# A cross-attention layer: the scores in stretches of two, three and three pairs, and what moves with them

## The reference, cut to what matters

```python
# x (8, 64, 512); ctx (8, 1601, 512); mask (8, 1601); 16 heads of 32
q = split_heads(layernorm(x) @ q_w.T + q_b)
k = split_heads(ctx @ k_w.T + k_b)
v = split_heads(ctx @ v_w.T + v_b)
scores = where(mask > 0, -inf, einsum("bhqd,bhkd->bhqk", q, k) / sqrt(32))
x = x + merge_heads(softmax(scores) @ v)                      # cross attention

h = layernorm(x)
q = h @ W_q.T
x = x + (q @ h.T) @ h                                         # per batch of 64 tokens

h = layernorm(x)
top_v, top_i = top_k(h @ gate_w + gate_b, 2)                  # 2 of 8 experts
x = x + sum over experts of weight * (relu(h @ w1[e] + b1[e]) @ w2[e] + b2[e])
```

## Time and profile before

| | us |
|---|---|
| median of 3 runs | 1223.51 |
| lowest and highest of them | 1223.32, 1225.69 |
| the profiled execution, its own time | 1225.0 |
| its span, from first to last instruction | 1223.2 |
| PE busy in the span | 1200.1 (98%) |
| DVE, ACT, POOL busy | 842.1, 697.7, 213.6 |

### The profile page before, as it was taken

How to read it: one execution, slowest core, us unless ns; L and a number is a source line. 1 busy time by engine, 2 the same in 40 slices (tenths; PEclk the granted TensorE clock), 3 DMA queues, 4 the chain that set the end, 5 groups by cost and what they waited for, 6 DMA issues and landing times.

```text
span 1223.2 us, 25806 instructions
## 1 busy us (share of the span) xinstructions
PE 1200.1 (98%) x10197; PEld 1122.2 (92%) x10197; DVE 842.1 (69%) x2154; ACT 697.7 (57%) x1266; POOL 213.6 (17%) x239
## 2 busy tenths in 40 slices
PE   7999999999999999999999999999999999999997
PEld 6899999999999999999999999999879898899896
DVE  6656666566665666666566666777789887887876
ACT  6455545645654564564455456455656676687772
POOL 0004202410420251051023105101112000000012
PEclk9999999999999999999999999999999999999999
DMA  8102200220220031022003002200318777768663
GB/s 286 55 1 92 85 1 2 95 82 1 92 84 1 3 118 58 1 92 84 1 28 119 31 2 92 98 1 2 114 69 285 245 253 262 251 226 283 234 206 122
DMA packets 61059, 127.19 MB, mean 104 GB/s; under 512 B 3644, under 2 KB 21192, under 8 KB 60824
## 3 DMA queue, kind: packets, MB, share of 16 engines
q1 hardware_dynamic: 58776, 118.97, 28.6%
q0 software_dynamic: 2176, 6.72, 1.5%
HBM read 120.01 MB, written 14.32 MB: 110 GB/s over the span
## 4 chain that ended last, share of the span: by engine, by line
PE 90%; DVE 6%; ACT 2%; DMA 1%; issue 1%; SPq 0%; DVEq 0%
PE ptp L948 26%; PE work L948 22%; PE work L1335 8%; PE ptp_pv L1118 6%; PE work L986 6%; PE work L1337 3%; PE ptp L1358 2%; PE ptp L1361 2%; PE ptp L1359 2%; PE ptp L1360 2%; PE ptp L1362 2%; DVE kk_lo L1498 2%; ACT kk_hi L687 1%; PE work L1101 1%; DVE pt L1617 1%; PE work L955 1%
## 5 line engine op out<-in xcount | busy, mean ns | idle before, releaser
L948 PE MATMUL ptp<-vw_hi,cx_hi 128*128 128x256 f32 x832 | 242.2, 291 | 0.0
L948 PE MATMUL ptp<-vw_lo,cx_hi 128*128 128x256 f32 x832 | 235.7, 283 | 0.0
L948 PE MATMUL ptp<-vw_hi,cx_lo 128*128 128x256 f32 x832 | 235.7, 283 | 0.0
L948 PE MATMUL work<-cx_hi,kw_hi 128*128 128x400 f32 (+1 forms) x504 | 175.8, 349 | 1.3 <-DVE cx_lo L1519 1.3
L948 PE MATMUL work<-cx_hi,kw_lo 128*128 128x400 f32 (+1 forms) x504 | 173.6, 344 | 0.0
L948 PE MATMUL work<-cx_lo,kw_hi 128*128 128x400 f32 (+1 forms) x504 | 173.4, 344 | 0.0
L948 PEld LDWEIGHTS ptp<-vw_hi,cx_hi 128*128 128x128 f32 x832 | 159.5, 192 | 13.8 <-issue 12.7
L948 PEld LDWEIGHTS ptp<-vw_lo,cx_hi 128*128 128x128 f32 x832 | 159.6, 192 | 0.0
L948 PEld LDWEIGHTS ptp<-vw_hi,cx_lo 128*128 128x128 f32 x832 | 159.6, 192 | 0.0
L1498 DVE SCALAR_TENSOR_TENSOR kk_lo<-work,biasT,kk_hi 128x400 fp32r<-128x400 f32 (+1 forms) x128 | 79.5, 633 | 115.0 <-ACT kk_hi L687 114.9
L687 ACT ACTIVATE kk_hi<-work,biasT 128x400 fp32r<-128x400 f32 (+1 forms) x128 | 75.1, 595 | 127.2 <-PE work L948 124.5
(11 more groups left out here) (301 smaller groups left out, 2601.0 us busy)
## 6 DMA issues: line engine op xcount, KB each, us to landing
w1raw<-in_w SPq DMA_DIRECT2D x32, 1024.0 KB, 6.1
w2raw<-in_w SPq DMA_DIRECT2D x32, 1024.0 KB, 5.3
raw<-in_ctxT SPq DMA_DIRECT2D x31, 832.0 KB, 6.5
pr<-in_mask SPq DMA_DIRECT2D x8, 800.5 KB, 4.4
xrow<-x_rows SPq DMA_DIRECT2D x7, 256.0 KB, 5.3
y_rows<-y_out_rows POOLq DMA_DIRECT2D x7, 256.0 KB, 3.7
xs<-in_x SPq DMA_DIRECT2D x1, 1024.0 KB, 9.8
qwraw<-in_qwT SPq DMA_DIRECT2D x1, 1024.0 KB, 8.8
```

What stands on the lines that cost most here:

```text
L948: last = pe.matmul(dst, lhs(i, c), rhs(j, c), start=(c == 0 and (i, j) == (0, 0)), stop=(c == n - 1 and (i, j) == (1, 0)))
```

## The change

- The eight score pairs of a half are in stretches of 2, 3 and 3 pairs in place of 2, 2, 2 and 2. The third pair of a stretch is written to `ptp[2]` and `pv` (ring banks 4 and 5), with a wait that the sums of the half before have been drained.
- All seven value items are now ahead of the last stretch, and `t` is behind it. The first three transposed blocks of a half all use ptp 0 and 1 (`PAIR_OF` 2, 2, 2), so `t` waits for v6 to be drained; the third block waits until the first two have been drained; and the first weighing of a half waits until the scores in `ptp[2]` and `pv` have been drained.
- The exponentials of the last row block come behind the first key item, and the last part of the context conversion (`ctx_hi` of part 3) comes behind those exponentials, where it was behind v6.
- `query_blocks` comes behind key item 3, where it was behind the last score tile of a half.
- In the last half, `n` lies between v4, v5 and v6; the query products 0, 1 and 2 are made there (two ahead of the first `w`, one between the two), each as 4 products of 384 columns; only product 3 is left behind the attention. `t` stands ahead of the last score pair.

```diff
@@ -62,34 +62,34 @@
         k = [] if h and last else [("k", 1 - h, j) for j in range(2 * NKC)]
-        s = [[("s", 4 * h + 2 * i + rt, j) for j in (2 * u, 2 * u + 1) for rt in range(2)]
-             for i in range(2) for u in range(2)]
+        pairs = [[("s", 4 * h + 2 * i + rt, j) for rt in range(2)] for i in range(2) for j in range(NKC)]
+        s = [sum(pairs[low:high], []) for low, high in SCORE_WINDOWS]
         e = [("e", 4 * h + r, 0) for r in range(4)]
...
             norms = [("m", 0, j) for j in range(EARLY)]
-            steps += s[0] + v[0:1] + norms[0:1] + v[1:2] + s[1] + e[0:1] + v[2:3] + norms[1:2] + e[1:2] + v[3:4]
-            steps += norms[2:] + s[2] + v[4:6] + s[3] + t
             turned, queried = [("n", 0, j) for j in range(EARLY)], [("q", 0, m) for m in range(EARLY_Q)]
-            steps += v[6:] + e[2:] + turned + w[:1] + queried + w[1:]
+            steps += s[0] + v[0:1] + norms[0:1] + v[1:2] + norms[1:2] + v[2:3] + s[1] + e[0:1] + v[3:4] + norms[2:] + e[1:2]
+            steps += v[4:5] + turned[:2] + v[5:6] + turned[2:] + v[6:] + s[2][:4] + t + s[2][4:] + e[2:]
+            steps += queried[:2] + w[:1] + queried[2:] + w[1:]
             continue
-        steps += s[0] + v[0:2] + s[1] + e[0:1] + v[2:3] + e[1:2] + v[3:4] + s[2] + v[4:6] + s[3]
-        steps += t + e[2:3] + v[6:] + e[3:]
+        steps += s[0] + v[0:3] + s[1] + e[0:1] + v[3:4] + e[1:2] + v[4:] + s[2] + t + e[2:3]
         if last:
             a, r = [("a", 0, j) for j in range(EARLY)], [("r", 0, j) for j in range(EARLY)]
-            steps += k[:1] + a[:1] + k[1:2] + r[:1] + a[1:2] + k[2:3] + r[1:2] + a[2:] + k[3:4] + r[2:] + k[4:5] + [("l", 0, 0)] + k[5:6]
+            steps += k[:1] + e[3:] + a[:1] + k[1:2] + r[:1] + a[1:2] + k[2:3] + r[1:2] + a[2:] + k[3:4] + r[2:] + k[4:5] + [("l", 0, 0)] + k[5:6]
         else:
-            steps += k[:6]
+            steps += k[:1] + e[3:] + k[1:6]
         steps += w[:1] + k[6:] + w[1:]
...
 EARLY = TT - 1
-EARLY_Q = 1
+EARLY_Q = 3
 EARLY_B = 2 * EARLY
...
+SCORE_WINDOWS = [(0, 2), (2, 5), (5, 2 * NKC)]
 STEPS = [steps_of(False), steps_of(True)]
@@ -106,7 +106,7 @@
-FILLED = (["q0_1", "att3", "b1", "q0_2", "q0_3", "turn0_3", "pre0", "pre1", "pre2", "own0", "own1", "own2", "q1a", "q1", "pre3",
+FILLED = (["q0_3", "att3", "b1", "turn0_3", "pre0", "pre1", "pre2", "own0", "own1", "own2", "q1a", "q1", "pre3",
            "own3", "turn1_0", "turn1_1", "turn1_2", "logits0", "turn1_3", "earlier0", "logits1", "earlier1", "total", "places", "weights",
@@ -125,7 +125,7 @@
 NEXT_TURNS = {1: (4, 5), 3: (6, 7), 5: (8,), 8: (11, 12), 10: (13,)}
-PAIR_OF = [3, 3, 2, 0, 1, 2, 0, 1, 2, 1, 2, 0, 1, 2]
+PAIR_OF = [2, 2, 2, 0, 1, 2, 0, 1, 2, 1, 2, 0, 1, 2]
@@ -174,12 +174,16 @@
         if kind == "s":
-            banks.append(scored % 4)
+            banks.append(scored)
             scored, others, late = scored + 1, 0, False
-        elif kind == "w":
+            continue
+        if kind in "vkanq":
+            scored = 0
+        if kind == "w":
             others, late = 0, True
...
             plain = others % 4 if others < 4 or last else 2 + others % 2
+            plain = 2 * j % 4 if kind == "q" else plain
             banks.append(2 if last and (kind, j) == ("k", 5) else plain)
@@ -202,7 +206,7 @@
     other = max(m for m in range(len(RING[0])) if BANKS[0][m] == bank)
-    return NW * b + FIRST_K + max(ITEMS[0].index(RING[0][other]) + 1 - NW, bank - 3)
+    return NW * b + FIRST_K + max(ITEMS[0].index(RING[0][other]) + 1 - NW, min(bank - 3, 0))
@@ -235,6 +239,7 @@
         sums = [ptp[2], pv]
+        ring = work + sums
@@ -775,10 +780,12 @@
                         kv_item(b, last, step)
-                    if kind == "v" and a == 1 and j in LAST_READ and not last:
+                    if kind == "v" and a == 1 and j in LAST_READ and j < TPH - 1 and not last:
                         ctx_hi(b + 1, LAST_READ[j])
...
                         exponentials(b, a)
+                    if step == ("e", 7, 0) and not last:
+                        ctx_hi(b + 1, LAST_READ[TPH - 1])
                     for j in turns(step):
@@ -824,12 +831,10 @@
             w1_part(0, 0, 0, True)
-            early_query(1)
+            early_query(C - 1)
             act.wait_ge(m_full, filled("b1"))
...
             root(3, range(EARLY, TT))
-            for m_ in range(2, C):
-                early_query(m_)
             turned(0, EARLY, yb[1])
@@ -979,11 +984,13 @@
                     pe.wait_ge(qbd_done, (2 * b + a // 4 + 1) * 2 * HPC)
-                pe.wait_ge(w_free, before_bank(b, last, both[1]))
+                pe.wait_ge(w_free, max(before_bank(b, last, step) for step in both))
+                if bank_of(last, both[0]) == 4:
+                    pe.wait_ge(pv_free, 4 * b + 2 * (a // 4) + 1)
                 for i, j in PASSES:
...
                         rows = slice(2 * HD * rt, 2 * HD * (rt + 1))
-                        ins = pe.matmul(wide(work[bank_of(last, both[rt])], k), qbd[i][rows, cc, :],
+                        ins = pe.matmul(wide(ring[bank_of(last, both[rt])], k), qbd[i][rows, cc, :],
                                         kk[j][rows, cc, keys(k)], start=(i, j) == (0, 0), stop=(i, j) == (1, 0))
@@ -1007,7 +1014,7 @@
                 kind, a, k = step
-                bank = (ptp if spare(step) else work)[bank_of(last, step)]
+                bank = (ptp if spare(step) else ring)[bank_of(last, step)]
                 if kind == "s":
@@ -1028,11 +1035,8 @@
                     pe.wait_ge(ld2[1], 16)
-                    for t in range(EARLY):
-                        pe.wait_ge(w_free, count(b, last, ("n", 0, t)))
-                        tokens = slice(t * P, (t + 1) * P)
-                        ins = plain(bank[:, tokens], lambda c: wq2[:, c, k * P:(k + 1) * P], lambda c: hT[:, c, tokens])
-                    ins.then_inc(w_full, 1)
+                    pe.wait_ge(w_free, count(b, last, ("n", 0, EARLY - 1)))
+                    early_query(k, bank).then_inc(w_full, 1)
@@ -1080,9 +1084,9 @@
                 if jj == 0:
-                    pe.wait_ge(pv_free, 4 * b + 2 * h + 1)
+                    pe.wait_ge(w_free, count(b, last, ("v", h, TPH - 1)))
                 if jj == 2:
-                    pe.wait_ge(w_free, count(b, last, ("v", h, TPH - 1)))
+                    pe.wait_ge(pt_lo, NPT * b + j + PTD)
                 if jj in (3, 4):
@@ -1110,6 +1114,8 @@
                     pe.wait_ge(pv_free, 4 * b + g + 1)
+                if j % (2 * TPH) == 0:
+                    pe.wait_ge(w_free, before_pair(b, last, 2, ("w", g, 0)))
                 for n in range(min(2, KT - first)):
@@ -1165,15 +1171,13 @@
             pe.wait_ge(w_free, count(LASTB, 1, ITEMS[1][-1]))
-            early_query(1, work[0]).then_inc(m_full, 1)
+            early_query(C - 1, work[2]).then_inc(m_full, 1)
             pe.wait_ge(pt_lo, NPT * B + PTD)
...
             pe.transpose(pv[:, 0:P], b1r[:], ident[:]).then_inc(m_full, 1)
-            for m_ in range(2, C):
-                early_query(m_, work[m_ - 1]).then_inc(m_full, 1)
             pe.wait_ge(ln2, TT)
@@ -1641,7 +1645,7 @@
                     kind, a, j = step
-                    for i in turns(step) if not (last and step == ("t", 2, 0)) else ():
+                    for i in turns(step):
                         pt_item(b, last, i)
@@ -1659,13 +1663,10 @@
                         item(b, last, step)
-                    if last and step == ("v", 1, TPH - 1):
-                        for i in turns(("t", 2, 0)):
-                            pt_item(b, last, i)
-                    if step == ("s", 3, NKC - 1):
+                    if step == ("k", 1, 3):
                         query_blocks(b, 1)
-                    if step == ("s", 7, NKC - 1) and not last:
+                    if step == ("k", 0, 3):
                         query_blocks(b + 1, 0)
```

## The result

The changed kernel takes 1231.73 us (median of 4 runs, 1230.96 to 1233.21), the kernel before beside it 1223.61: a ratio of 1.0064, 95% interval 1.0048 to 1.0080. It is slower by 8 us where 1222.7 was forecast. Its profiled execution took 1231.47 us, with a span of 1229.7 (before: 1225.0 and 1223.2), so the two traces differ by 6.5 us. These are to be found. That stretch is thus in some executions and not in others, and most of the missing 1.6 us may be it.

What follows compares the result with a forecast made beforehand. PE, busy 98% of the span, was taken as the bound. Terms -6.1 + 2.0 - 3.36 + 5.06 + 0.75 = -1.6 us gave 1222.7 us; own range 1221.2 to 1224.2, 8-in-10 range 1219.2 to 1226.0.

Steps and rivals of the forecast that it cites:

- The stretches: Score stretches on PE, four made three in each of 16 halves: 0.38 us less per half, -6.1 us.
- New waits in the ordinary halves: `t`, k4, the moved context part and `query_blocks` in ordinary halves: PE pays no new wait, 0 us.
- First half of the last batch: Turn 4 of the first `w` waits for DVE's low part of k5: +2.0 us, bounds 0 and 3.5.
- The clock falls at both new pauses: Rival, chance 0.10: clock also falls at turn 4 (+1.3), full +2.7 behind the attention (+1.0): 1225.0 us.
- Last half: First `w` loses its `hT` wait and slow clock, -3.36 us; two more query products ahead cost together +5.06.
- the slow stretch: First `w` of the last half, before the change: half clock behind the 1.93 us wait, 1.26 us.
- Behind the attention: After the last `w`: 0.95 us saved, PE pauses 4.4 us, half clock over self scores +1.7; +0.75 in all.
- the middle between two sums: Forecast of 1222.7 us, between 1223.4 from the trace's own time and 1221.9 from the median.

Runs made afterwards that it cites:

- x7: Changed kernel with scores in four stretches again (2, 2, 1 and 3 pairs): 1238.17 us, ratio 1.0131 to the kernel before.
- x1: Changed kernel with POOL's four `xs + vb` additions moved ahead of batch 3's `ctx_lo`: 1227.29 us, ratio 1.0029.
- x5: Changed kernel with two query products in the last half, both ahead of the first `w`, product 2 behind the attention: 1231.62 us, ratio 1.0067.
- x9: Changed kernel with two query products in the last half, one ahead of the first `w`, one between the two: 1231.75 us, ratio 1.0060.
- x10: Changed kernel with 16 constant products ahead of PE's wait for the last tokens' norm: 1230.20 us, ratio 1.0042.
- x11: Changed kernel with `query_blocks` back behind the last score tiles and 24 memsets added to DVE's program: 1222.08 us, ratio 0.9985.
- x8: Memsets added early in DVE's program: 24 in the changed kernel, 1229.78 us (1.0045); 2 in the kernel before, 1227.45 us (1.0022).
- x12: As x11, with 16 constant products behind the attention too: 1219.59 us, ratio 0.9962.
- x13: Changed kernel with POOL's additions earlier, the last batch's `query_blocks` behind key product 6, 24 memsets and 16 constant products: 1219.40 us, ratio 0.9961.

## Why the prediction was wrong

- *The stretches*, -6.1: right. 0.75 to 0.77 us a batch, and +6.4 when undone (x7).
- *New waits in the ordinary halves*, 0: right for `t`, k4 and the context part. **Here is the step that failed**: "`query_blocks` (0.95 + 1.23 = 2.2 us on DVE) now lies between k3's and k4's low part; k4's is 0.6 late, k5's on time. 0." The 2.2 us were read where POOL stood idle, and carried to a place where in one batch POOL's additions run. There the first five of the eight operations took 5.73 us (4.48 + 1.25). The wait that the forecast put at nothing was 3.14 us; with the clock behind it the price is 4.9 us in the trace, 4.4 by x1. I had followed DVE's, ACT's and PE's queues past the moved step, and POOL's only for the context part. The Trainium skill ("SBUF — State Buffer", Who interferes with whom) has the rule: a VectorE copy in its fast mode, or an operation with two SBUF inputs, and a GpSimd operation that reads SBUF keep each other out for a whole instruction. The trace agrees: 1.1 us on the mean of a copy beside additions of 1.26 each, 1.25 for the one subtraction with two SBUF inputs that met the last addition, and nothing lost by operations that read one operand from PSUM (value drains beside the additions 0.42, score tiles beside a `cx_lo` 0.57, both in x1). Whether these copies ran in the fast mode no run shows.
- *First half of the last batch*, +2.0: 2.09 of wait, right. The whole is +2.6: +2.0 and +1.1 of clock, less some 0.5 that the stretches and other small terms give. The rival *The clock falls at both new pauses* was right for this place in this execution, +1.1 where it said +1.3; x1's run shows such a wait without it.
- *Last half*, -3.36 + 5.06: +1.4 against +1.7, and against +1.3 with the stretches' 0.38 of that half: right. But 1.26 of the -3.36 is the slow stretch, which the kernel before does not have in every execution. What I took for a price of products was right only beside the waits that they cover (x5, x9).
- *Behind the attention*, +0.75: +0.77, right; the pause was 4.32 us where 4.4 were forecast, and the clock's part 1.8 us where 1.7 were taken (x10).
- *Missing from the sum*: the end of the run, +3.4, which the forecast did not look at since nothing in it was edited. The Trainium skill ("Runtime: NRT & Kernel Launch", Instruction fetch mechanics) says that a jump out of the blocks at hand has to wait for its code, and that crossing a border costs little. The first fits (2.83 us behind the branch in the kernel before); for the second the measurement decides: 2.7 to 3.1 us here.

Between the -1.6 forecast and the +6.5 of the trace lie 8.1 us: the stall of batch 3 makes 4.9, the end 3.4, the clock at turn 4 1.1; a start 1.1 us earlier goes the other way. With the two causes out, x11 stands at 1222.08, where the whole had been forecast at 1222.7. That this is so near is in part luck: x11 has a wait of 1.0 us in the last batch where the forecast counted 2.0, and the forecast was the middle between two sums.

What stays open is when the clock falls behind a wait of 2 or 3 us. Among the traces of kernels with the wait of 3.1 us in batch 3 it fell in eight of nine; with the wait of 2.1 us at turn 4 of the last batch in seven of nine; behind the 1.93 us of the kernel before in two of three. This seems to be much of the scatter between executions: the four times of x8's changed kernel go from 1225.89 us at a mean granted clock of 0.996 to 1230.82 at 0.992, while x12 and x13, which have no such wait, stay within 1.1 and 0.7 us at 0.999.

## What to carry to other kernels

A duration belongs to the place where it was read: before a step of VectorE is moved, look in every batch at what GpSimd does beside the new place, above all for work that is in one batch only. A change of a few instructions can move a border of the code onto the end of the run; when a small change comes out some 3 us wrong with an untouched middle, compare the last records, and pad the program with real instructions to see. And price a piece of work on the bound engine only together with the waits that it covers.

## What was not expected of the hardware

- Four copies of 32 x 128 took 4.48 us beside GpSimd's additions, one copy per addition; 0.95 us with GpSimd idle, 1.45 with the end of one GpSimd instruction beside the first.
- Two instructions more in DVE's program, executed in the first 5 us, made the run 3.1 us longer, all of it in the end (4.53 to 8.08 us in the traces of x8).
- Behind a pause of 4.32 us the self scores took 4.07 us, with the pause filled 2.68; 3.6 us of constant products in it were enough.
- The same wait of 2 or 3 us brought TensorE's clock down in most executions and not in all, 1.1 to 1.8 us each time.
